# A graph layer with an expert stage: edge rows gathered once and multiplied by fours, mixing spread over tiles, and a small GpSimd write behind every gather

## The reference, cut to what matters

```python
xn = layernorm(x)
neigh_mean = segment_sum(xn[src], dst) / max(deg, 1)
gnn = l2norm(relu(concat([xn, neigh_mean]) @ W + b))
x = x + gnn + mix(xn)                 # linear attention, 4 heads of 32
x = x + experts(layernorm(x))         # top 2 of 8, hidden width 1024
```

## Time and profile before

| | us |
|---|---|
| median of 3 runs | 2065.89 (2065.57 to 2066.7) |
| span of the profiled execution | 2267.2 |
| layer norm, z, tables | 0 to 90 |
| stage A of the walk | 90 to 660 |
| context part | 660 to 747 |
| stage B of the walk | 747 to 1350 |
| last adds, routing, scatters | 1350 to 1577 |
| expert tiles | 1577 to 2267 |

### The profile page before, as it was taken

How to read it: one execution, slowest core, us unless ns; L and a number is a source line. 1 busy time by engine, 2 the same in 40 slices (tenths; PEclk the granted TensorE clock), 3 DMA queues, 4 the chain that set the end, 5 groups by cost and what they waited for, 6 DMA issues and landing times. The chain is left out here.

```text
span 2267.2 us, 34877 instructions
## 1 busy us (share of the span) xinstructions
PE 1666.7 (74%) x9448; PEld 1326.2 (58%) x9449; DVE 1305.5 (58%) x3579; ACT 899.5 (40%) x1840; POOL 1177.1 (52%) x1203
## 2 busy tenths in 40 slices
PE   6656566665756666787666663555999999999997
PEld 5534343443434434434444342443999999999996
DVE  6434343443434557776777667753666666666663
ACT  6501010110110233333444336642666666666663
POOL 3466666666656666666666543663333333333333
PEclk9867777776768877889787885557999999999998
DMA  7433333333333465656666536745565565555554
GB/s 203 122 111 106 100 104 100 103 105 96 103 95 91 149 222 178 195 180 190 184 206 191 181 110 199 257 167 156 122 137 129 128 136 128 133 130 134 132 126 93
DMA packets 193411, 325.02 MB, mean 143 GB/s; under 512 B 34453, under 2 KB 136865, under 8 KB 192286
## 3 DMA queue, kind: packets, MB, share of 16 engines
q0 software_dynamic: 80912, 208.73, 35.0%
q1 hardware_dynamic: 103574, 112.56, 16.2%
q10 hardware_dynamic: 8824, 2.61, 0.6%
HBM read 244.30 MB, written 80.26 MB: 143 GB/s over the span
## 5 line engine op out<-in xcount | busy, mean ns | idle before, releaser
L1245 DVE TENSOR_TENSOR acc_lent<-acc_lent,bank 128x258 f32 x832 | 350.0, 421 | 527.5 <-remote 267.6
L677 POOL DMA_INDIRECT G<-z_d,edge_tabs_lent x416 | 404.3, 972 | 294.2 <-issue 119.6
L677 POOL DMA_INDIRECT w2s_lent<-z_d,edge_tabs_lent x416 | 402.0, 966 | 182.3 <-issue 117.8
L1684 PE MATMUL bank<-G,S_lent 128*128 128x258 f32 x832 | 286.0, 468 | 156.3 <-DVE acc_lent L1245 86.2
L1684 PE MATMUL bank<-w2s_lent 128*128 128x258 f32 x832 | 293.6, 478 | 114.7 <-issue 71.9
L1684 PEld LDWEIGHTS bank<-G,S_lent 128*128 128x128 f32 x832 | 166.8, 226 | 240.6 <-issue 167.7
L1684 PEld LDWEIGHTS bank<-w2s_lent 128*128 128x128 f32 x832 | 171.9, 233 | 203.0 <-issue 139.0
L717 POOL DMA_INDIRECT out_dram<-G,acc_lent x112 | 178.3, 1592 | 201.3 <-DVE G L1572 126.3
L1551 DVE TENSOR_TENSOR acc<-w1s,acc 128x512 fp32r<-128x512 f32 x224 | 155.0, 693 | 204.7 <-ACT acc L995 182.5
L1008 ACT ACTIVATE G<-bank,acc_lent 128x256 f32<-128x256 f32 x448 | 188.0, 471 | 195.6 <-DVE acc L1592 84.7
L1888 PE MATMUL bank<-w2s,acc 128*128 x896 | 261.5, 292 | 1.8 <-DMA edge_tabs<-w2lo_d 1.8
(11 more groups left out here) (294 smaller groups left out, 3134.6 us busy)
## 6 DMA issues: line engine op xcount, KB each, us to landing
S<-w2lo_d POOLq DMA_DIRECT2D x56, 512.0 KB
edge_tabs<-w2lo_d POOLq DMA_DIRECT2D x56, 512.0 KB
acc_lent<-bucket_d SPq DMA_DIRECT2D x56, 266.0 KB, 2.9
bu_d<-w2s_lent SPq DMA_DIRECT2D x98, 128.0 KB
w2s_lent<-bu_d SPq DMA_DIRECT2D x12, 768.0 KB
w1s<-in_L_ffn_W_dram SPq DMA_DIRECT2D x8, 1024.0 KB
w2s_lent<-in_L_ffn_W_dram SPq DMA_DIRECT2D x32, 256.0 KB
w2hi_d<-w2s_lent SPq DMA_DIRECT2D x32, 256.0 KB
```

Source lines behind the costliest of these rows:

```text
L677: pool.indirect_dma_start(out=G_half[half][:, k, 0:D], out_offset=None, in_=z_d[:, :], in_offset=bass.IndirectOffsetOnAxis(ap=srcT[:, step ...
L1245: dve.tensor_tensor(to, to, bank[k % 4][:, 0:ACCW], ALU.add).then_inc(s["acc_done"], 1)
L1684: pe.matmul(bank[k % 4][:, 0:ACCW], S_half[half][:, k // S_GROUP, k % S_GROUP, :], G_half[half][:, k, :], start=True, stop=True).then_inc( ...
```

## The change

1. An edge row is gathered once. Four rows are a quad (QUADS = 196), and a ring of 8 quads (32 slots instead of 16) keeps them. A turn is one quad for one node tile. There are TURNS = 196 + 48 = 244 of them. A quad that straddles two tiles is used from the ring in two turns. TensorE reads its slot from a table into registers (8 values at a time), as GpSimd and VectorE do with theirs.
2. In a turn TensorE runs four matmuls that add up in one PSUM bank, and signals once. VectorE adds once, and builds S (128x512) once. Up to four turns are open (DEPTH). In stage A and the context part a follow() stands behind every turn. In stage B there is none.
3. GpSimd waits, before a quad, until the quad two before it has landed, and then raises quads_in, on which TensorE waits (IN_FLIGHT = 2). It waits for the ring slot by a count of turns.
4. Behind each of the 784 gathers GpSimd writes 8 zeros for each partition into a spare corner (rest, an iota).
5. Stage A has one or two turns for each mixing tile (90 turns over 48 tiles), the context part 6, stage B three for each tile (147), and one is left. In stage B the product with M2 of tile t-1 stands in tile t, behind its first turn, and its norm and scaling too. The bias fold starts at tile 10 instead of 16.
6. The tables are built otherwise (two indirect DMAs of quads instead of seven of rows, another set of transposes), and buffers have moved. The load of the second routing group waits for b1_mm, and that of the third for the last add.

```diff
+            def rest(n):
+                until(pool, s["rested"], n - 3)
+                iota_f(idle[:, n % 4, :], [[0, 8]], 0, 0).then_inc(s["rested"], 1)
+            def landed(q):
+                pool.wait_ge(g_in[q % IN_FLIGHT], 16 * QUAD * (q // IN_FLIGHT + 1))
+                pool.sem_inc(s["quads_in"], 1)
+            for q in range(QUADS):
+                if q >= RING:
+                    if q % REGS == 0:
+                        _, frees = nc.values_load_multi_w_load_instructions(...)
+                    pool.wait_ge(s["p_ready"], frees[q % REGS] & COUNT)
+                if q >= IN_FLIGHT:
+                    landed(q - IN_FLIGHT)
+                for k in range(QUAD):
+                    row = QUAD * q + k
+                    pool.indirect_dma_start(out=ring_rows[:, row % (RING * QUAD), 0:D], ...)
+                    rest(row)
...
+            def turn(j):   # TensorE
...
+                pe.wait_ge(s["quads_in"], needs[j] & COUNT)
+                pe.wait_ge(s["s_built"], j + 1)
+                until(pe, s["acc_done"], j + 1 - DEPTH)
+                for k in range(QUAD):
+                    rows = ring[:, k * ACCW:(RING - 1) * QW_RING + (k + 1) * ACCW]
+                    m = pe.matmul(bank[j % DEPTH][:, 0:ACCW], S_of[j % DEPTH][:, k, :], rows[:, ds(bases[j], ACCW)],
+                                  start=(k == 0), stop=(k == QUAD - 1))
+                m.then_inc(s["p_ready"], 1)
+                if j < B_FIRST:
+                    follow()
...
+            def turn(j):   # VectorE
...
+                dve.wait_ge(s["p_ready"], j + 1)
+                until(dve, s["acc_done"], j)
+                to = acc_flat[:, ds(places[j], ACCW)]
+                dve.tensor_tensor(to, to, bank[j % DEPTH][:, 0:ACCW], ALU.add).then_inc(s["acc_done"], 1)
+                if j + DEPTH < TURNS:
+                    build_S(j + DEPTH)
...
+            for t in range(NT):   # stage B on TensorE
...
+                qu(t)
+                turn(mine[0])
+                if t:
+                    mix_out(t - 1)
+                turn(mine[1])
+                if 0 <= f < 2 * EXPERTS:
+                    bfold(f // 2, f % 2)
+                turn(mine[2])
+                turn_q(t)
```

More of the change, by code:

```diff
@@ L26 @@
 NOWHERE = 1 << 20
-STEPS_J = 7
-STEP_BLOCK = 8
-S_GROUP = 4
+QUAD = 4
+QUADS = EROWS // QUAD
+RING = 8
+IN_FLIGHT = 2
+DEPTH = 4
+REGS = 8
 X_AHEAD = 8
@@ L1178, in step_counts @@
[L1178 to L1181 removed]
+                quads_i = quads_flat.bitcast(I32)
+                first, last = quads_flat[:, 0:NT], quads_flat[:, NT:2 * NT]
+                dve.tensor_copy(Lr, bank[6][:, 0:NT])
+                dve.tensor_copy(quads_i[:, 0:NT], bank[6][:, 0:NT])
@@ new lines, in step_counts @@
+                L.after(dve.tensor_scalar(quads_i[:, NT:2 * NT], bank[7][:, 0:NT], float(QUAD - 1), None, ALU.add))
+                dve.tensor_tensor(has, bank[7][:, 0:NT], Lr, ALU.is_gt).then_inc(s["tables_ready"], 1)
+                L.after(dve.tensor_scalar(quads_i, quads_i, 2, None, ALU.logical_shift_right))
+                L.after(dve.tensor_copy(quads_flat, quads_i))
+                L.after(dve.tensor_tensor(turns_of, last, first, ALU.subtract))
+                L.after(dve.tensor_tensor(turns_of, turns_of, has, ALU.mult))
@@ L1233, in walk @@
-            def walk(i, half, hooks={}):
-                _, places = nc.values_load_multi_w_load_instructions(
-                    acc_at[0:1, ds(STEP_BLOCK * i, STEP_BLOCK)], engines=[mybir.EngineType.DVE], min_val=0, max_val=NT * PAYW,
-                    skip_runtime_bounds_check_because="a count of at most NT tiles, times the width of one")
-                for k in range(STEP_BLOCK):
-                    step = STEP_BLOCK * i + k
-                    if k % S_GROUP == 0:
-                        until(dve, s["p_ready"], step - S_GROUP)
-                        build_S(2 * i + k // S_GROUP + 2, 1 - half, k // S_GROUP)
-                    dve.wait_ge(s["p_ready"], step + 1)
-                    until(dve, s["acc_done"], step)
-                    to = acc_flat[:, ds(places[k], ACCW)]
-                    dve.tensor_tensor(to, to, bank[k % 4][:, 0:ACCW], ALU.add).then_inc(s["acc_done"], 1)
-                    if k in hooks:
-                        hooks[k]()
@@ L1251, in late_weights @@
+            for j in range(DEPTH):
+                build_S(j)
+            dve.memset(kmax, -3e38)
+            z_stored(dve)
+            dve.memset(ring_rows[:, :, D:ACCW], 1.0).then_inc(s["consts_dve"], 1)
             def late_weights():
@@ L1279, in _ @@
                     LATE_AT + 3: lambda: bias_rows(1), LATE_AT + 4: lambda: bias_rows(2)}
-            def a_hooks(i):
-                hk = {7: lambda: kmax_tile(i)}
+            for i in range(NT - 1):
+                mine = turns_of_a(i)
+                turn(mine[0])
                 if i in late:
-                    hk[3] = late[i]
-                return hk
-            blocks(lambda i, h, turn: walk(i, h, a_hooks(i)), 0, NT - 1)
+                    late[i]()
+                for j in mine[1:]:
+                    turn(j)
+                kmax_tile(i)
             kmax_tile(NT - 1, TAIL)
@@ L1304, in sub_k @@
                                   ALU.subtract).then_inc(s["ek_sub"], 1)
-            A2 = NT - 1
-            blocks(lambda i, h, turn: walk(i, h, {0: lambda: sub_k(i - A2)}), A2, A2 + 6)
+            for g in range(6):
+                sub_k(g)
+                turn(CTX_FIRST + g)
             sub_k(6, 1, TAIL)
@@ L1673, in follow @@
                 pe.matmul(bank[spare][:, 0:P], before[:, :], ones_b[:, :], start=True, stop=True)
[L1675 to L1690 removed]
+            bases, needs = {}, {}
@@ L1707, in _ @@
             turn_a(0)
-            blocks(lambda i, h, turn: walk(i, h, turn, {2: lambda: turn_a(i + 1), 6: lambda: kv(i)}), 0, NT - 1)
+            for i in range(NT - 1):
+                mine = turns_of_a(i)
+                turn(mine[0])
+                turn_a(i + 1)
+                for j in mine[1:]:
+                    turn(j)
+                kv(i)
             kv(NT - 1)
@@ L1727, in ctx_mm @@
                 m.then_inc(s["ctx_mm"], 1)
-            A2 = NT - 1
-            blocks(lambda i, h, turn: walk(i, h, turn, {7: lambda: ctx_mm(i - A2)}), A2, A2 + 6)
+            for g in range(6):
+                turn(CTX_FIRST + g)
+                ctx_mm(g)
             ctx_mm(6, 1, TAIL, True)
```

476 lines of the change are left out of this document (254 added, 222 removed).

## The result

The changed kernel takes 2032.5 us (median of 4 runs, 2029.1 to 2034.1). The kernel before took 2065.7 us in the same comparison. The ratio is 0.9841, 95% interval 0.9823 to 0.986. So the change is worth 33 us, where I had said 138. The direction is right and the time lies in the range, but the main term of the sum is wrong.

A forecast was written before the change was run, and what follows sets the result against it. GpSimd's gather issue, then late TensorE signals, bound the walk. Gathers -61, writes +86 and waits -176 us cut it from 1270 to 1119; these 151 us, scaled to 138, took 2065.9 to 1928 us, range 1860 to 2090.

The forecast's parts named there:

- GpSimd's issue is the first bound: In the walk: gathers 1.25 us apart on GpSimd set the pace; 832 of them make 1060 of 1256 us.
- Late TensorE signals the second: In the walk: during long unbroken gather runs TensorE's signals come late, taking about 15% of the walk.
- the waits that stay at 20 us instead of 196: GpSimd's waits in the walk: fall from 196 to 20 us, -176 us in the profile.
- My own sign of being wrong: Signs against the forecast: remaining pauses, spacing over 1.5, or a profile 150 us shorter while the median is not.
- Scaling: Whole kernel: the profile's saving of 151 us, times 0.911 (median over span), becomes 138 us.
- only in the profiled execution: Rival for GpSimd's waits in the walk: unprofiled runs have prompt signals, so the change is slower, 2101 us; chance 0.15.
- Gathers: GpSimd's queue in the walk: 832 gathers become 784, 48 x 1.274 = 61 us less, all on the path.
- The write: Behind each gather on GpSimd: 784 x 0.11 = 86 us more; from nothing up to 196 us.
- Landing: GpSimd's wait before a quad: landing after 2.8 us is covered by 5.5 us of issue; late ones within 20 us.
- TensorE, VectorE and the pace: In the walk: neither engine is the bound; a stage A tile takes 9.3 us, a stage B tile 12.4.
- Ends: Tables, first gather and 14 us tail stay; SyncE's two added waits cost two or three microseconds, left in the range.

## Why the prediction was wrong, point by point

*What bounds the walk.* "GpSimd's issue is the first bound" was right, and two writes instead of one show it. "Late TensorE signals the second, which take about 15% of the walk" was wrong for the runs that are timed.

*The failed step* is the term "the waits that stay at 20 us instead of 196", -176 in the sum. It took the waits of one profiled execution for the kernel's own. In the kernel's next two profiles the walk's loss was 40 and 38 us instead of 216, of which some 11 were waits for TensorE beyond the usual gap. The change then raised the loss to 51 instead of lowering it, so the term is about +11 where I had -176. The warning stood in my own text: a span 201 us over the median, and waits of 196. I argued that "all waits would have to vanish". They did. My own sign of being wrong came too, a profile much shorter while the median is not: the profiled span fell by 235 us, the median by 33.

*Luck in the direction.* The same sum with the waits' term at a few microseconds of landing waits and the write at my 86 us is the rival's 2101 us, slower than before. That the change came out faster, and inside my range, is owed to a second error against the first: the write costs about 20 us of spacing and not 86. Between the second profile of before and that of the changed kernel, 48 gathers fewer give -60 us, the wider spacing 783 x 0.025 = +20, the loss +12, and the stretches behind the last gather about +1, together -28 in the span (2059.9 to 2032.1).

*Scaling.* "Scaled x 0.911" spread the excess evenly over the kernel. It was not even: 181.7 of 207.3 us lay in the walk. Where the excess is concentrated in the stage that one argues about, scaling doesn't correct for it.

*The rival "only in the profiled execution"* had the right mechanism and the wrong time, 2101. Its price for the write was the mis-sized term. With the gathers as I had them and the other two as measured, it reads 2066 - 61 (gathers) + 12 (write) + 21 (landing) = 2038, within 6 us of the result.

*Gathers,* -61: right in size, but only together with the new structure. Alone they brought 40 us; with quads and three in flight, without the write, the kernel is 0.9679 of before, 63 us less by the medians and 66 by the ratio.

*The write,* +86, bounds 0 and 196: the value is 12 us in the changed kernel, 7 in the kernel before, 21 where nothing else waits. The spacing shows 0.022 to 0.028 us, near the lower bound. I had named that bound ("if it fits into the 0.305 us") and took the iotas at the start, which have no gather behind them. They were the same operation in another place. For the upper end I had also weighed a lock of the ports that GpSimd and VectorE share. The Trainium skill's "SBUF — State Buffer", section "SBUF: two separate sides", names that lock for VectorE operations in a two-port mode, and for those with two SBUF inputs only against a GpSimd operation that reads SBUF. The rows of the iota name no input, so a build of S, which has two, was the wrong operation to price it by. No run here shows a wait that matters: the writes take 0.15 us (91.52, 92.80) in stage A and 0.16 at the mean in stage B, beside a VectorE that is busy 341 of 585 us, and the longest of the 784 takes 0.39.

*Landing,* "covered", with the late quads in the 20 us: wrong by about 21 us. I compared a landing of 2.8 us with the 5.5 us that a quad takes to issue. The first figure lacked the signal and the restart (4.0 in all), and the second was right on average but the tail of the landings reaches past it. That explains some 9 of the 23 us of lost spacing; the rest came with the same wait in a form that the trace of before couldn't show. The way from before to after in ratios is 0.9679 (structure and 48 gathers fewer), +0.0108 (two quads in flight instead of three), +0.0054 (the write). These add up by construction. What is independent is that the first is 63 to 66 us where 48 gathers at 1.285 are 62, and that the second stands in the loss too, as 23 us.

*TensorE, VectorE and the pace.* TensorE isn't the bound: in the changed kernel it waits for quads.

```profile
PE bank L1768 <- POOLq L680: 210.9, 97, 7.0
```

VectorE's load falls as said. The same stretch of the walk in the second profile of before and in the changed kernel (columns as in the earlier trace rows):

```profile
520.00:1105.00 585.00, 430.37 (x1646) 276.06 (x1645) 435.99 (x1169) 212.97 (x384) 443.49 (x450) 0.90 0.65 199
```

```profile
520.00:1105.00 585.00, 448.75 (x1647) 315.56 (x1646) 341.29 (x910) 210.54 (x375) 501.29 (x855) 0.89 0.64 197
```

VectorE goes from 436 to 341 us, GpSimd from 443 to 501 with the writes in it. A tile of stage A takes (520.2 - 100.0)/48 = 8.8 us by the adds (forecast 9.3), one of stage B (1139.6 - 565.5)/49 = 11.7 (forecast 12.4). Both forecasts were too long by the price of the writes. But the 11.9 and 12.3 us that I set beside them were from the disturbed execution: a block of stage A of before takes 10.1 us on average in its second profile (the 49 copies at line 866 start from 103.5 to 586.4 us).

*Readings.* Two readings of the earlier trace rows were a little off: GpSimd is 4 to 6 tenths busy in the slices of the walk, not 5 to 7, and TensorE's granted clock is 6 to 9 tenths there, with the fives behind it. Nothing in the sum hangs on them.

*Ends.* From the last add to the end the kernel before has 2059.9 - 1178.3 = 882 us and the changed one 2032.1 - 1147.2 = 885. The two or three microseconds for SyncE's waits were right.

What stays open: what made the profiled execution of the earlier trace rows different. It wasn't seen again, so nothing could be tried on it. TensorE's mean granted clock was lower in it too, 0.829 against 0.886 and 0.877 in the next two profiles; whether that is a cause or a consequence isn't shown. That a long unbroken run of gathers delays signals isn't supported: the same runs of gathers are in the second and third profile, with signals within 0.05 us.

## What to carry to other kernels

Before a wait is given a price, set the profiled span beside the median of the runs. Where they differ by as much as the waits that one wants to remove, profile again: it costs one execution, and here it would have taken a term of 160 us (176 x 0.911) out of the sum. On an engine that is bound by issue, a small instruction is priced by the change in spacing in that very place, not by its duration elsewhere. And a wait for one's own earlier transfers is to be measured from issue to restart, against the slowest landings, and by a run with one more group in flight: here it was worth 21 us, beside the 33 of the whole change.

## What the runs showed that I had not expected

- A write of 8 elements for each partition, placed behind an indirect DMA on GpSimd, takes 0.15 us and lengthens the spacing by 0.022 to 0.028 us. A second one costs 0.081.
- With one quad in flight, 4.0 us pass from the start of an indirect DMA to the start of the next one that waits for its landing, where the landing itself is at 2.8.
- With two quads in flight, GpSimd pauses between the first and the second gather of every 28th quad, where no wait for a landing stands. In the changed kernel these are the gathers that start at 236, 383, 532, 690, 840 and 993 us, exactly 112 gathers apart; the pause is 2.0 us over the usual spacing, and 5.0 at 690. One of them:

```profile
234.06 0.15 POOL L613 IOTA small<- 128x8 f32 x1
236.34 0.95 POOL L692 DMA_INDIRECT w2s_lent<-z_d,edge_tabs_lent  x1 [2.14 <-issue]
```

  They come at the same gathers without the write (238, 382, 527, 682, 831, 983 us, 15 us in all) and with two writes, where 112 gathers take 160 us instead of some 150. So they are tied to a place in the program and not to time. None of this form is in the kernel before. With three in flight one of 1.15 us is left (521.6 us), so they make 14 of the 23 us between two and three in flight.

- The semaphore events in the traces show where such a pause comes from. GpSimd's sequencer, which takes up instructions ahead of the engine, has 1.95 us at the median between the end of one wait for a landing and the start of the next (kernels without the write). While it issues quad 28 this takes 7.9 us with two in flight (230.6 to 238.4 us), and 7.35 with three as well (223.5 to 230.8). But with two in flight its wait before quad 28 ends 3.5 us before the quad's first gather starts, with three 8.5 us before. So the third quad in flight doesn't remove the delay. It gives the sequencer the lead that hides it. With three in flight there are seven such delays, 27 quads apart, of 5.9 to 10.3 us. What holds the sequencer there the traces don't say, and it stays open.
